# Head scores of 13 small-head attentions as stacked bf16 matmuls: three parts of q and k, 48 rows per head, built through DRAM

## The reference

```python
def _attn(q, k, v, mask):                       # H; HD = 8, 16 heads
    scores = jnp.einsum('bqhd,bkhd->bhqk', q, k) / np.float32(np.sqrt(HD))
    scores = jnp.where(mask[:, None, None, :], jnp.float32(-jnp.inf), scores)
    w = jax.nn.softmax(scores, axis=-1)
    return jnp.einsum('bhqk,bkhd->bqhd', w, v)
for i in range(6):
    xn = _adaln(x, noise_emb, n1_w[i], n1_b[i])
    q, k, v = split(xn @ qkv_w[i].T); q, k = _rope(q), _rope(k)
    x = x + _attn(q, k, v, src_mask).reshape(B, L, D) @ so_w[i].T
    xn = _adaln(x, noise_emb, n2_w[i], n2_b[i])
    q = _rope(xn @ cq_w[i].T); k = _rope(context @ ck_w[i].T); v = context @ cv_w[i].T   # 77 keys
    x = x + _attn(q, k, v, ctx_mask).reshape(B, L, D) @ co_w[i].T
    xn = _adaln(x, noise_emb, n3_w[i], n3_b[i])
    x = x + (gelu(xn @ f1_w[i].T + f1_b[i]) @ f2_w[i].T + f2_b[i])
```

## Time and profile before

| | us |
|---|---|
| median of 3 runs | 7536.24 (7529.18 to 7542.61) |
| the profiled execution, its own time | 7551.09 |
| its span | 7549.2 |
| busy over the span: PE, PEld | 5957.4, 4368.6 |
| busy: DVE, ACT, POOL | 4808.1, 2846.9, 1030.7 |
| granted TensorE clock, mean of the core | 0.834 |

### The profile page before, as it was taken

One profiled execution on the slowest core, in us unless ns is written; L12 is line 12 of the kernel. 1 busy time (PEld: TensorE's weight loads), 2 busy tenths in 40 slices (PEclk: granted clock), 3 DMA queues, 4 the chain that ended last, 5 costly groups with the idle time before them and its releaser, 6 DMA issues. The chain is left out here.

```text
span 7549.2 us, 189229 instructions
## 1 busy us (share of the span) xinstructions
PE 5957.4 (79%) x79705; PEld 4368.6 (58%) x79720; DVE 4808.1 (64%) x16917; ACT 2846.9 (38%) x4943; POOL 1030.7 (14%) x924
## 2 busy tenths in 40 slices
PE   4454568898878788787799688888888888888887
PEld 3343446666666577676577466556565565565655
DVE  6777964544558766666544586575675765765864
ACT  2221224444424311111112255456455554554563
POOL 1113521211200200000000110110111111011101
PEclk7667879999989655555699898999989989989998
DMA  1000000000000000000000000000000000000000
GB/s 33 1 0 3 1 29 1 1 1 1 1 5 2 6 3 3 3 3 3 24 1 1 19 2 2 11 2 2 11 2 7 6 2 7 6 2 11 2 2 15
DMA packets 61231, 44.75 MB, mean 6 GB/s; under 512 B 22521, under 2 KB 56125, under 8 KB 60227
## 3 DMA queue, kind: packets, MB, share of 16 engines
q1 hardware_dynamic: 60355, 32.26, 1.6%
HBM read 30.14 MB, written 2.10 MB: 4 GB/s over the span
## 5 line engine op out<-in xcount | busy, mean ns | idle before, releaser
L261 DVE TENSOR_REDUCE peak<-ps 128x8 f32<-128x1024 f32 (+1 forms) x832 | 817.0, 1024 | 264.1 <-PE ps L183 263.6
L303 ACT ACTIVATE e<-ps,H_lowT_c 77x1024 f32<-77x1024 f32 x384 | 405.6, 1105 | 271.7 <-PE ps L207 271.7
L303 ACT ACTIVATE e<-ps,H_lowT_s 128x1024 f32<-128x1024 f32 x384 | 407.1, 1111 | 250.6 <-PE ps L207 250.6
L221 PEld LDWEIGHTS ps<-e,H_vt 128*32 128x32 f32 (+1 forms) x12288 | 326.6, 113 | 262.0 <-ACT e L303 145.3
L221 PE MATMUL ps<-e,H_vt 128*32 128x128 f32 (+1 forms) x12288 | 443.2, 286 | 23.6 <-DVE xs L281 17.7
L2482 POOL TENSOR_TENSOR H_rstd<-H_veps,neghalf 128x4 f32<-128x4 f32 (+1 forms) x146 | 161.0, 1103 | 2130.3 <-DVE H_veps L2478 2130.3
L207 PE MATMUL ps<-H_qr,H_km 32*128 32x128 f32 (+1 forms) x12288 | 435.3, 281 | 0.0
L207 PEld LDWEIGHTS ps<-H_qr,H_km 32*128 32x128 f32 (+1 forms) x12288 | 420.7, 174 | 16.8 <-issue 3.7
L2176 ACT ACTIVATE F_ex<-ps,F_nm 16x77 f32<-16x77 f32 x256 | 81.3, 318 | 835.0 <-DVE F_nm L2087 835.0
L311 ACT ACTIVATE oT<-ps 128x512 f32<-128x512 f32 x416 | 248.4, 597 | 368.0 <-PE ps L221 368.0
L183 PE MATMUL ps<-H_km,H_qr 32*128 32x512 f32 (+1 forms) x3072 | 354.4, 529 | 0.0
(11 more groups left out here) (650 smaller groups left out, 13789.8 us busy)
## 6 DMA issues: line engine op xcount, KB each, us to landing
G_w<-in_L_ffn_w SPq DMA_DIRECT2D x16, 256.0 KB
H_f<-in_L_xcond_f_w SPq DMA_DIRECT2D x12, 256.0 KB
H_nw<-in_L_xcond_n_w SPq DMA_DIRECT2D x21, 128.0 KB, 2.1
A_cond<-in_cond SPq DMA_DIRECT2D x1, 2048.0 KB
out_x<-x_all SPq DMA_DIRECT2D x1, 2048.0 KB, 8.7
ctx_rows<-in_ctx SPq DMA_DIRECT2D x1, 1232.0 KB
D_wq<-in_L_xcond_attn_wq SPq DMA_DIRECT2D x2, 512.0 KB
D_wk<-in_L_xcond_attn_wk SPq DMA_DIRECT2D x2, 512.0 KB
```

Of the source, the lines that this page charges most:

```text
L221: last = nc.tensor.matmul(ps[PAD_COLS * s:PAD_COLS * (s + 1), FLAT, r * S:(r + 1) * S], vt_of(u)[0:keys, QUAD * r + s, :], e[0:keys, half, ...
L261: last = nc.vector.tensor_reduce(peak[:, HL * half:HL * (half + 1)], view, AX.X, ALU.max, negate=True)
L303: nc.scalar.activation(e[0:keys, half, :], ps[0:keys, AGAIN[half]:AGAIN[half] + 2, :].rearrange("p b t -> p (b t)"), ACT.Exp, bias=low(u) ...
```

## The change

Scores come from bf16 matmuls instead of f32 ones. Each of q and k is written as a sum of three bf16 parts, high, middle and low: ACT copies the high part to `row_parts` (`row_high`), POOL subtracts it in place (`row_left`), ACT copies the middle part (`row_middle`), POOL forms the low part (`row_low`). SP saves the parts to a DRAM tensor `scratch` (`save_parts`) and reads them back as **stacks** (`read_stack`): head by head, six blocks of eight rows, so that 48 rows hold q parts (0,1,2,0,1,0) against k parts such that one matmul over 48 rows sums six of the nine products. Head t lies in partitions 0 to 47 of the stack, head 8+t in partitions 64 to 111. In H row 49 is 1 in q and the mask in k. Half h of a unit is now heads 4h to 4h+3 and 8+4h to 8+4h+3. The masked copies `km` and their operations are gone, the factor 1/sqrt(8) goes to the exponential, the shifts are laid by `own` (a constant) against one copy of `shift`. The halves are ordered apart: half 1 (banks 2, 3 and then 4, 5) first.

```diff
+        def save_parts(sp, G, i, wide):
+            sp.wait_ge(sem["parts_ready"], 2 * G + i + 1)
+            for c in range(3):
+                at = c if i == 0 else 2 - c
+                sp.dma_start(scratch[i, G, :, at, :, 0:wide], row_parts[:, i, c, 0:wide]).then_inc(sem[("q_saved", "k_saved")[i]], 16)
+        def read_stack(sp, G, i, stack, wide):
+            sp.wait_ge(sem[("q_saved", "k_saved")[i]], SAVES * (G + 1))
+            for j in range(2):
+                at = 64 * j
+                for n, first in ((3, 0), (2, 0), (1, 0)) if i == 0 else ((3, 0), (2, 1), (1, 2)):
+                    sp.dma_start(stack[at:at + HD * n, G % 2, :, 0:wide],
+                                 scratch[i, G, HL * j:HL * (j + 1), first:first + n, :, 0:wide].rearrange("t c r n -> (c r) t n")
+                                 ).then_inc(stacked(i, G), 16)
+                    at += HD * n
...
-                for r in range(QUAD):
-                    last = nc.tensor.matmul(view(r), q_of(u)[rows(r), :], km_of(u)[rows(r), :, :],
-                                            start=(low_of is None), stop=True, skip_group_check=True)
+                if N >= 1:
+                    pe.wait_ge(sem[("half_peaked", "upper_peaked")[half]], N)
+                if N >= 2 and half == 0:
+                    pe.wait_ge(sem["exp_done"], 2 * N - 2)
+                for s in range(QUAD):
+                    for j in range(2):
+                        last = nc.tensor.matmul(ps[:, 2 * half + j, s * S:s * S + keys], q_of(u, j, QUAD * half + s), k_of(u, j, QUAD * half + s),
+                                                start=True, stop=True, skip_group_check=True)
...
+            def lay_shift(u, half):
+                if half == 1:
+                    pe.wait_ge(sem["shift_ready"], N + 1)
+                    if N >= 1:
+                        pe.wait_ge(sem["exp_done"], 2 * N - 1)
+                else:
+                    if u + 1 < units:
+                        pe.wait_ge(sem["half_peaked"], N + 2)
+                    if N >= 1:
+                        pe.wait_ge(sem["exp_done"], 2 * N)
...
+            for k in range(units + 1):
+                if k < units:
+                    scores(k, 1)
+                if k >= 1:
+                    lay_shift(k - 1, 1)
+                if k >= 2:
+                    values(k - 2, 1)
+                if k < units:
+                    scores(k, 0)
+                if k >= 2:
+                    values(k - 2, 0)
+                if k >= 1:
+                    if meanwhile:
+                        meanwhile(k - 1)
+                    again(k - 1, 1)
+                else:
+                    keep_clock(12, FLAT)
+                if k >= 2:
+                    flip(k - 2)
+                if k >= 1:
+                    lay_shift(k - 1, 0)
+                    again(k - 1, 0)
+                if k < units:
+                    turn_peaks(k)
...
-                nc.vector.tensor_tensor(shift[:], ps[:, PEAKS, 0:S].unsqueeze(1).broadcast_to([128, QUAD, S]),
-                                        own_row[:].unsqueeze(2).broadcast_to([128, QUAD, S]), ALU.mult).then_inc(sem["shift_ready"], 1)
+                nc.vector.tensor_copy(shift[:], ps[:, PEAKS, 0:S]).then_inc(sem["shift_ready"], 1)
...
+                            for r in (SELF, CROSS):
+                                for g in range(NG):
+                                    if r == CROSS and g == 1:
+                                        row_deviations(pool, NG - 1, group(NG - 1))
+                                    for i in ((1, 0) if r == CROSS else (0, 1)):
+                                        add_products(r, g, i)
+                                    if g in (2, 4):
+                                        lefts(r, (g - 2) // 2)
+                                    if g in (3, 5):
+                                        lows(r, (g - 3) // 2)
```

More of the change, by code:

```diff
@@ L163, in keep_clock @@
                                  ones_b[:].unsqueeze(1).broadcast_to([128, 2, S]), start=True, stop=True, skip_group_check=True)
-        def small_tensor(pe, first, units, keys, q_of, km_of, vt_of, low_of, ready, ready_values, meanwhile=None, area_free=None):
-            rows = lambda r: slice(ROWS * r, ROWS * (r + 1))
-            def scores(u):
+        scratch = nc.dram_tensor("scratch", (2, 2 * NG, NH, 3, HD, U * S), BF16, kind="Internal").ap()
+        row_parts = pT[:].rearrange("p b h s -> p (b h s)")[:, 0:3 * U * S].bitcast(BF16).rearrange("p (i c n) -> p i c n", i=2, c=3)
@@ L170, in scores, with small_tensor @@
+        def small_tensor(pe, first, units, keys, depth, queries, keyed, vt_of, ready, ready_values, meanwhile=None, area_free=None):
+            tall = lambda j: slice(64 * j, 64 * j + depth)
+            q_of = lambda u, j, t: queries[tall(j), ((first + u) // U) % 2, t, (u % U) * S:(u % U + 1) * S]
+            k_of = lambda u, j, t: keyed[tall(j), ((first + u) // U) % 2, t, (u % U) * keys:(u % U + 1) * keys]
+            def scores(u, half):
                 N = first + u
-                ready(u)
+                if half == 1:
+                    ready(u)
@@ L230, in flip @@
                 last.then_inc(sem["o_flipped"], 1)
-            scores(0)
-            keep_clock(12, FLAT)
-            for u in range(units):
-                turn_peaks(u)
-                if u + 1 < units:
-                    scores(u + 1)
-                if u:
-                    values(u - 1, 0)
-                    values(u - 1, 1)
-                if meanwhile:
-                    pe.wait_ge(sem["shift_ready"], first + u + 1)
-                    meanwhile(u)
-                again(u)
-                if u:
-                    flip(u - 1)
+            for k in range(units + 1):
[13 more added lines that the diff above has]
+                    again(k - 1, 1)
+                else:
+                    keep_clock(12, FLAT)
[6 more added lines that the diff above has]
+                    turn_peaks(k)
+            values(units - 1, 1)
             values(units - 1, 0)
-            values(units - 1, 1)
             if meanwhile:
@@ L1585, in stage_attn_experts, with _ @@
                     mine = lambda g: slice(g * U * S, (g + 1) * U * S)
+                    rows_of = lambda i, g: (qr, kr)[i][:, mine(g)]
+                    @block.sync
+                    def _(sp):
+                        for g in range(NG):
+                            for i in range(2):
+                                save_parts(sp, g, i, U * S)
+                            if g >= 2:
+                                sp.wait_ge(sem["again_done"], 2 * U * (g - 1))
+                            for i in range(2):
+                                read_stack(sp, g, i, stacks[i], U * S)
                     @block.tensor
```

311 lines of the change are left out of this document (170 added, 141 removed).

## The result

The changed kernel takes **8109.98 us** (median of 4 runs, 8089.43 to 8135.8); the kernel before took 7532.71 on the same chip (7526.61 to 7542.61). The ratio is **1.0775**, 95% interval 1.0748 to 1.0802: some 577 us slower. The forecast was 7,463 with a range up to 7,650, so it was wrong in sign and in size. The profiled execution has a span of 8087.6 us and a mean granted clock of 0.733, against 7549.2 and 0.834.

The account below looks back on a forecast made before the run. PE was taken to bound all 13 attentions. Terms -77 - 23 - 10 + 24 + 13 = -73 us gave 7,478 against the profiled execution, stated as 7,463 because that execution lies 15 above the median; range 7,290 to 7,650.

Parts of the forecast that it names:

- rival 5: Whole kernel: PE's granted clock falls, as in one stretch granted 0.50; 7,700 us and more; chance 0.05.
- PE bounds all attentions; two self rounds 9.9 us, cross 9.6: All 13 attentions: PE sets the round; per unit self 5.37 to 4.96 us, cross 4.91 to 4.79.
- Eights 0.36 and 0.34: Blocks of eight bf16 matmuls on PE: 0.36 us for scores and scores again, 0.34 for shifts; bounds 0.25 and 0.59.
- rival 3: Attention rounds: PE becomes slower, a block of eight taking 0.43 to 0.44 us; 7,650 us; chance 0.28.
- The 0.68 behind ACT goes, 0.3 behind the shift copy comes: Self round on PE: the 0.68 us wait for ACT's exponential disappears; a 0.3 us wait for DVE's shift copy appears.
- Self -77, cross -23, E -10: Gains in us from shorter rounds: 192 self units 77, 192 cross units 23, 32 E units 10.
- Projection +24, starts +13: Losses: 2 us in each of 12 projection phases (POOL's added operations), 1 us of pipeline filling at 13 starts.
- DMAs hidden at 0: Stack saves and reads: land at 15 to 16 us under a group's four rounds of 19.8 us, cost 0.
- Rival 2: Attention rounds: bf16 blocks cheaper than taken, six eights shrink by 150 us, about 7,320 us in all; chance 0.15.

Follow-up runs that it names:

- before_bf16_again2: Kernel before with the 16 f32 matmuls of the second scores replaced by bf16 ones times ones, leaving out q and k there: 7630.88 us, ratio 1.015.
- fill12b: Changed kernel with 12 bf16 matmuls of ones (256 columns each) added in every round, ahead of the wait for the copied shift: 7916.18 us, ratio 1.054.
- kick: Changed kernel with 48 matmuls of 256 columns in one piece, once in each attention, in its ninth round: 8218.05 us, ratio 1.0905.
- together: Changed kernel with the two halves of the first scores, and those of the values, one behind the other again: 8240.34 us, ratio 1.094.
- two_stacks: Changed kernel without saves and reads of the stacks from the third group on in the decoder layers (14 of 16 groups): 8059.85 us, ratio 1.0698.
- fill6: Changed kernel with 6 bf16 matmuls of ones (256 columns each) added in every round, ahead of the wait for the copied shift: 8402.03 us, ratio 1.1129.
- fill_f32b: Changed kernel with one f32 matmul of 384 columns of ones (four passes) added in every round: 8542.95 us, ratio 1.1336.

## Why the prediction was wrong

**The step that failed** is rival 5, "the clock falls", at 0.05, and behind it the assumption under every term of the sum, that PE would stay at 1.00 in the attentions. It was weighed by one row of another stretch ("20.87 of 30 us busy kept 0.94"). A busy share doesn't bear on it: the cross round of the changed kernel is busy for 19.97 of 20 us and is kept at 0.50. What the runs showed in its place: one lighter block takes the cross attentions of before to 0.50 (before_bf16_again2, +1.5%), and twelve added matmuls bring those of the changed kernel back to 1.00 (fill12b). The price that I named, "7,700 and more", gave only a floor, some 400 us under the result. Before itself had the warning: in the earlier trace rows a cross attention at 0.50 with PE busy for 19.45 of 20 us stayed there for 40 us of full rounds. That round was near the border, as before_bf16_again2 shows, and the change took streaming out of it.

Step by step:
- *PE bounds all attentions; two self rounds 9.9 us, cross 9.6.* Right at full clock: 9.73 (with 0.59 and 0.47 of waiting for DVE in one of the two), and 9.47 for the two cross rounds of kick. Where the clock is 0.50, 220.65 / 31 = 7.12 per cross unit.
- *Eights 0.36 and 0.34.* Measured 0.32 to 0.33 at full clock, below the value and far from rival 3's 0.43; break-even was 0.39. Rival 3, and with it the draining of TensorE on a change of tiling mode that the Trainium skill states (TensorEngine Tiling (Array Packing), Key Properties), costs no more than forecast: 8 x 0.055 / 2 = 0.22 of streaming in 0.33 leaves 0.11 per block, what f32 blocks of the earlier trace rows pay too. How much of the 0.11 is a drain no run shows.
- *The 0.68 behind ACT goes, 0.3 behind the shift copy comes.* Right in kind: DVE's copy takes 0.29 (forecast 0.28), and "together" brings the wait for ACT back. But the wait for the copy doesn't stand in every round: of the three rounds that begin at 4401.31, 4405.76 and 4411.04 only the last has it, 0.47, and over the whole execution, much of it at 0.50 where PE's own blocks are longer, the waits (us in total, times, longest) are:

```profile
PE ps L253 <- DVE shift L337: 30.2, 59, 0.7
```

- *Self -77, cross -23, E -10.* Measured +77, +357, +51. With the rounds at full clock, 31 x (5.37 - 4.87) is 15.5 us per self attention and 31 x (4.91 - 4.74) 5 per cross one: six of each make some 125, and less the 53 outside some 70, an estimate (without E) of what the change would gain if the clock held by itself. Forecast without E were 63.
- *Projection +24, starts +13.* All outside the attentions +53. From a self attention to the next cross one it is 12 us in six layers, from a cross one to the next self one 36 in five; in the latter part of it is the clock again (4812.4 to 4966.2 was granted 0.87, its like before, 4696.7 to 4843.8, 0.91), since these stretches start at 0.50. How the rest divides between POOL, the wait for a save and the start isn't shown.
- *DMAs hidden at 0.* Wrong in mechanism, small in price. PE stands before the first scores of some groups, with no releaser named, behind a stack whose last reads were issued 8 us earlier and while DMA traffic runs out (120 GB/s in 4420 to 4424, 49 in 4424 to 4428); that it waits for the stack is inferred from the program's order, and two_stacks agrees, whose page of waits has none of this kind:

```profile
4418.18 1.45 SPq L2670 DMA_DIRECT2D H_k_stack<-pT  x2
4427.79 0.61 PE L228 MATMUL ps<-H_k_stack,H_q_stack 49*128 49x128 bf16 x8 [2.00 <-issue]
PE ps L228 <- issue: 33.0, 21, 5.0
```

  The last row is the waits' total over the whole execution: 33.0 us, 21 of them, the longest 5.0. I had reckoned with the rate of the output's store, 235 GB/s; the stretch 4412 to 4424 moved 120 to 191. Taking the stacks of 14 in 16 groups away brought 0.7%, some 58 us, part of it time at 0.50.
- *Rival 2* has 0.06 per eight in its sum where its text says 0.05; with what was measured, 0.36 less 0.33, it would be some 75 us instead of 150.
- *The 49th row and the small copies*: nothing in the runs separates the mask's share.

Was it only the clock? fill12b has some 1.4 us of added work in each of 416 rounds, has its attentions at 1.00 for most of their time (cross 179 to 204 us, self 184 to 202), and still beats the changed kernel; before_bf16_again2 shows the fall with one lighter block alone. What stays open is how much streaming a round must have, and in what form: fill6 and fill_f32b, with 0.6 to 0.7 us added, did not raise the clock in cross attentions, fill12b did, and all added matmuls use the full 128 rows and columns, which the round's own mostly don't. The runs that moved the clock multiply ones by ones in the block concerned; whether values matter wasn't tried. Nor was a version tried that keeps the changed self attention with its clock held, and the cross attention of before.

## What to carry over

Before taking matmul passes out of a round that PE bounds, look how near its clock is to falling: a stretch of before that was busy and yet granted 0.50 for tens of us was here the sign that the round was near the border, and then work saved on PE raised the price of all that was left (7.12 us per cross unit at 0.50, 4.74 at full clock). Read the granted clock of the very stretch beside the busy share, since at 0.50 the share looks best. And try to fill the stops at the start of each attention: 26 more matmuls of ones in each gave 0.8% here, in the kernel whose rounds hold the clock, and nothing in the other.

## What the runs showed of the hardware

- A busy PE is not a PE at full clock: 20.00 of 20 us busy at 0.50 (fill6), 17.96 of 20 at 1.00 (before_bf16_again2, self attention).
- More work can be faster: 8402 us with 6, 7916 us with 12 added matmuls per round; and less work slower: 7631 us with one block of the kernel before made lighter, ratio 1.015.
- How long the clock stays down after a stop differs for the same stretch of program: cross attentions of before are at 0.50 for some 40 us in four of six cases, for two rounds in the two others (164 to 165 against 154.0 us), and with the start filled for one round at most (151 to 153 us).
- In before_bf16_again2 the round with 128 keys gets back to 1.00 after one or two rounds and holds it, the same round with 77 keys stays at 0.50 (146 against 198 us). The latter follows a longer stop (3.07 to 3.11 us against 1.48).
- Eight bf16 matmuls of 128 columns on 64-row tiles of 49 rows take 0.33 us at full clock (4402.67 to 4402.99 above) and 0.54 at half (changed kernel, 4387.01 to 4387.56). With 77 keys as weights it is 0.35 (kick, 5312.60 to 5312.95) and 0.58 (4656.41 to 4656.99 above). At half clock a block isn't twice as long.
